# Squared leaky rectifier as two squares, a norm moved to ScalarE, scalings in one product

## The chip, the cores and the metric

One core of a Trainium2 chip runs the program. The metric is the device time of one execution in microseconds; the kernel before is given as the median of three runs, beside one profiled execution.

## What is computed

Two layers, each an attention-like part and an expert part, with a norm behind each. The change touches only the first part of layer 0, cut here to what matters:

```python
normed = _rms(x)
k, v, r = normed @ Wk.T, normed @ Wv.T, sigmoid(normed @ Wr.T)
# scan over the sequence of k*v -> wkv
x1 = x + mixer_scale * (r * wkv @ Wo.T)
h  = leaky_relu(_rms(x1) @ Wfc.T, negative_slope=0.5)
x2 = x1 + mlp_scale * (h * h @ Wmlp.T)
x3 = layernorm(x + x2)
# then layer 0's experts: 8, each token goes to 2 of them; then layer 1
```

x has 16 x 256 rows of 128; the hidden size of Wfc is 512. All of it is float32 here.

## The kernel before

Layer 0's first part runs over 8 chunks of 512 rows (4 tiles of 128). Its steps are software-pipelined by a table `AT` (line 34): the step numbered `u` is done for chunk k where u = 16 k + AT[name]. So a chunk's steps lie 16 apart, and the steps of up to six chunks are interleaved. Every engine runs the same list of slots in one written order (`program_order`, line 323) and does its own part of each slot; what it does in one slot it does in the order of the code. Nothing is reordered at run time: an instruction that waits holds everything behind it on its engine. From u = 64 on, slots of the experts of the first half of the rows stand between those of layer 0; then come the experts of the second half, the sums of the expert outputs, and layer 1's attention.

Seen modulo 16 from the large product `mlp` at step 2, TensorE does: logits and `mlp` (2), `fc` 1 (4), mix (6), `fc` 2 (7), the transpose of x (9), `fc` 3 (10), the transpose of x1 and ranks (12), k and v (13), the transpose of x3 (14), r (15), `fc` 0 of the next chunk (1). ScalarE does: half 0 (3), half 1 and exp (6), square 0 (7), half 2 (9), the squares of x1 for its norm and square 1 (10), the copy of xT (11), half 3 (12), square 2 (13), copies of x1T (14) and k (15), the squares of x, square 3 and the copy of x3T (0), the gate (1). VectorE: mixT (4), `x3_sums` (5), xn (6), x1 (8), the choice of two experts (8, 10), x3 (11), places (15), x1n (0), the scan (1), largest (2), and one `leaky` at 5, 8, 11 and 14. GpSimd: scatters of expert rows (2, 5, 8, 11; two DMAs each), the inverse roots (3, 9, 13) and `xx` (15).

The rectifier, for each of four 128-wide parts f of the hidden size: TensorE puts `fc` into PSUM bank 7 or 6 in turn (line 908); ScalarE writes its half to `z_half` (line 622, two buffers); VectorE takes the greater of the two, out of SBUF and PSUM, to `leaky` (line 759), which frees the bank; ScalarE squares that to `h_fc` (line 627). Then TensorE multiplies all four by `wmlp` into one bank, 16 products of 128x128x128 (line 922); one such product is two instructions, and so in the trace 32 a chunk.

The norm x3: VectorE adds the residual to `tmp` (line 763) and makes mean and variance (lines 766 to 769); GpSimd makes the inverse root (`inverse_root`, lines 475 and 477); VectorE subtracts and multiplies with both as scalars, four tiles a chunk (line 774). The two RMS scalings are four instructions each too (lines 714 and 754). `take` on TensorE (line 1995) holds a bank until its last reader has counted a semaphore up.

## Time and profile before

| | |
|---|---|
| median of 3 runs | 1436.43 us (1427.48 to 1438.81) |
| the profiled execution, its time | 1430.42 us |
| its span in the trace | 1428.6 us |
| TensorE busy | 1195.4 us (84%) |
| VectorE busy | 953.0 us (67%) |
| ScalarE busy | 733.5 us (51%) |
| GpSimd busy | 661.1 us (46%) |

The span is that of the instructions in the trace; the execution's time has 1.8 us around it. Engines in the rows: PE is TensorE (PEld its weight loads), DVE VectorE, ACT ScalarE, POOL GpSimd, SP the queue that issues most DMAs. Busy shares are over the whole span, of which layer 0's chunks are a small part and attention (from about 322 us on) the largest; the stretch of interest is read by itself.

### The profile page before, as it was taken

The numbers are of one execution on the slowest core, as the hardware profiler recorded it, in microseconds if no ns is written. First come the engines' busy times: TensorE is split into PE (matmuls) and PEld (weight loads), VectorE is DVE, ScalarE is ACT, GpSimd is POOL, SyncE is SP. The second block draws the span as 40 slices with busy tenths as digits, with TensorE's granted clock in tenths as the row PEclk, the third lists the DMA queues.
The fourth block names the chain that finished last, engine by engine and source line by source line (L and its number), as shares of the span: only waits on it lengthen the run. The fifth ranks groups of instructions, "written<-read, shape, count | busy, mean of one in ns | idle before, by whom it ended". The sixth has DMA issues, their size and how long they took to land.

```text
span 1428.6 us, 30595 instructions
## 1 busy us (share of the span) xinstructions
PE 1195.4 (84%) x11664; PEld 714.2 (50%) x11664; DVE 953.0 (67%) x2280; ACT 733.5 (51%) x1244; POOL 661.1 (46%) x1054
## 2 busy tenths in 40 slices
PE   5978786867676888999999989989999998999985
PEld 2545575654233344455545545455455555555554
DVE  4788542354468878787776768787786866747534
ACT  3654343334242466665655656566565655663541
POOL 2367442762268446364453626345462542543430
PEclk7999899987576899999998989999998999999887
DMA  9900366741010001101010110101011010110110
GB/s 341 356 16 32 114 206 201 223 137 42 16 35 25 15 7 42 33 14 38 10 45 3 44 32 15 37 11 45 20 28 33 14 45 4 44 42 18 23 36 8
DMA packets 69481, 87.53 MB, mean 61 GB/s; under 512 B 22062, under 2 KB 54104, under 8 KB 65880
## 3 DMA queue, kind: packets, MB, share of 16 engines
q1 hardware_dynamic: 65240, 77.18, 18.3%
q0 software_dynamic: 4096, 8.40, 1.9%
q8 instruction: 94, 1.54, 0.5%
q14 instruction: 51, 0.42, 0.1%
HBM read 52.16 MB, written 32.21 MB: 59 GB/s over the span
## 4 chain that ended last, share of the span: by engine, by line
PE 51%; DVE 27%; ACT 6%; issue 5%; POOL 4%; SPq 4%; DMA 2%; ACTq 0%; DVEq 0%; POOLq 0%
PE ps L1678 24%; PE ps L1758 11%; DVE mneg_e L1493 8%; PE ps L864 5%; PE ps L1781 4%; DVE mneg_l L1493 3%; POOL gathered L568 2%; DVE q L1548 2%; PE ps L960 2%; SPq L1137 2%; PE ps L1778 2%; DVE o_e L1591 1%; DVE x_all L847 1%; PE ps L1896 1%; DVE v_l L1668 1%
## 5 line engine op out<-in xcount | busy, mean ns | idle before, releaser
L1336 ACT ACTIVATE probs<-ps 128x1024 f32<-128x1024 f32 x384 | 389.3, 1023 | 231.5 <-PE ps L1678 230.8
L1493 DVE TENSOR_REDUCE mneg_e<-ps 128x2 f32<-128x512 f32 x512 | 335.8, 683 | 62.7 <-PE ps L1678 59.9
L1493 DVE TENSOR_REDUCE mneg_l<-ps 128x2 f32<-128x512 f32 x256 | 167.5, 685 | 63.9 <-PE ps L1678 62.4
L1678 PE MATMUL ps<-k_high,q_high 32*128 32x256 f16 x1024 | 163.6, 280 | 43.3 <-DVE mneg_e L1493 38.8
L1758 PE MATMUL ps<-probs,v_e 128*32 128x256 f32 x2048 | 139.7, 391 | 7.9 <-ACT v_e L1361 4.3
L1678 PE MATMUL ps<-q_high,k_high 32*128 32x256 f16 x1024 | 142.2, 278 | 3.6 <-ACT probs L1336 3.5
L1678 PE MATMUL ps<-q_low,k_high 32*128 32x256 f16 x1024 | 141.4, 275 | 0.0
L1678 PE MATMUL ps<-q_high,k_low 32*128 32x256 f16 x1024 | 140.4, 273 | 0.0
L1231 POOL CAST k_high<-k 128x512 f16<-128x512 f32 x64 | 39.8, 622 | 159.4 <-ACT k L1352 159.4
L1678 PE MATMUL ps<-kT,qT 32*128 32x256 f16 x512 | 76.7, 292 | 36.3 <-DVE mneg_l L1493 19.1
L1548 DVE SCALAR_TENSOR_TENSOR q<-ps,bq,pick 128x256 f32<-128x256 f32 x128 | 55.9, 478 | 72.5 <-PE ps L1678 72.5
L1276 POOL CAST routeT<-routeT 21x256 f16<-21x256 f32 x16 | 6.2, 387 | 195.0 <-ACT routeT L1424 195.0
L1678 PEld LDWEIGHTS ps<-k_high,q_high 32*128 32x128 f16 x1024 | 55.1, 93 | 82.4 <-DVE mneg_e L1493 58.2
L1289 POOL TENSOR_TENSOR on_e<-o_e,on_e 128x512 f32<-128x512 f32 x60 | 76.1, 1271 | 37.3 <-DMA on_e<-scratch_e 37.3
L551 POOL DMA_INDIRECT by_expert<-x_all,places x64 | 63.9, 998 | 52.0 <-DVE places L805 35.8
L1678 PEld LDWEIGHTS ps<-q_high,k_high 32*128 32x128 f16 x1024 | 48.9, 93 | 77.8 <-issue 52.0
L1758 PEld LDWEIGHTS ps<-probs,v_e 128*32 128x32 f32 x2048 | 54.0, 110 | 60.6 <-issue 22.7
L1758 PE MATMUL ps<-probs,v_l 128*32 128x256 f32 x1024 | 80.6, 440 | 1.1 <-DVE qkv L1561 0.3
L568 POOL DMA_INDIRECT gathered<-by_expert,places x64 | 62.2, 972 | 39.7 <-DMA by_expert<-y_tokens 22.6
L1678 PE MATMUL ps<-x5T,wq 128*128 128x256 f32 x256 | 74.7, 416 | 3.8 <-ACT k L1352 3.8
L1781 PE MATMUL ps<-x5T,wk 128*128 128x256 f32 x256 | 74.1, 417 | 0.0
L1236 POOL TENSOR_TENSOR k_low<-k,k_high 128x512 f16<-128x512 f32 x64 | 73.7, 1152 | 0.0
(245 smaller groups left out, 2501.5 us busy)
## 6 DMA issues: line engine op xcount, KB each, us to landing
by_expert<-expert_w SPq DMA_DIRECT2D x12, 1536.0 KB, 14.4
expert_w<-in_expert_w SPq DMA_DIRECT2D x48, 321.0 KB, 3.9
on_e<-scratch_e SPq DMA_DIRECT2D x60, 256.0 KB, 4.6
tokens<-by_expert SPq DMA_DIRECT2D x48, 128.0 KB, 2.6
by_expert<-y_tokens SPq DMA_DIRECT2D x48, 128.0 KB, 1.9
on_l<-scratch_l SPq DMA_DIRECT2D x128, 32.0 KB, 1.8
sums_l<-o_l SPq DMA_DIRECT2D x128, 2.0 KB
q_high<-shiftT_e SPq DMA_DIRECT2D x128, 2.0 KB
```

The costliest lines, as they stand in the source:

```text
L551: pool.indirect_dma_start(by_expert[g], bass.IndirectOffsetOnAxis(ap=places[:, n, at:at + 1], axis=0), x_all[:, at, :], None).then_inc(z.s ...
L568: pool.indirect_dma_start(gathered[:, k % 2, n, t, :], None, by_expert[g], bass.IndirectOffsetOnAxis(ap=places[:, n, k * CT + t:k * CT + t ...
L864: return pe.matmul(o, l, r, start=start, stop=stop)
L1231: pool.tensor_copy(k_high[:, b % 2, g], k32[:, g % 2]).then_inc(s.k16_ready, 1)
L1236: pool.tensor_tensor(k_low[:, b % 2, g], k32[:, g % 2], k_high[:, b % 2, g], ALU.subtract)\
L1289: pool.tensor_tensor(on_e[:, :, g], o_e[:, :, g], on_e[:, :, g], ALU.mult).then_inc(E.on_ready, 1)
L1336: act.activation(probs[:, probs_slot(r, i)].rearrange("p j s -> p (j s)"), s_banks(i).rearrange("p j s -> p (j s)"), ACT.Exp, scale=0.5 if ...
L1493: v.tensor_reduce(to, tiles(max_bank(k)), axis=AX, op=ALU.max, negate=True).then_inc(kind.max_used, 1)
L1548: last = v.scalar_tensor_tensor(q32[:, g % 2, c, :], x0[:, c * S:(c + 1) * S], bq[:, c, g:g + 1], pick[:, c, :], ALU.add, ALU.mult)
L1678: return pe.matmul(o, l, r, start=start, stop=stop)
L1758: last = pe.matmul(x1[ROW * j:ROW * (j + 1), to * S:(to + 1) * S], values, probs[:, probs_slot(r, first + 2 * t + j // 2), j % 2, c * S:(c ...
L1781: last = pe.matmul(x0[:, c * S:(c + 1) * S], wk[:, c, g, :], x5T[:, b % 2], start=False, stop=True, skip_group_check=True)
```

## The change

With z a part of `fc`, leaky(z) squared is z squared for z > 0 and (z/2) squared otherwise, and so (z/2)^2 + (sqrt(3/4) relu(z))^2. ScalarE now reads each part twice out of PSUM: Square with scale 0.5 to `z_square` (five buffers, since the product reads it a chunk later) and Relu with scale sqrt(0.75) to `z_half`; then it squares `z_half` to `h_fc` as before. VectorE's `leaky` is gone, and a bank is free with the second reading. TensorE adds the two squares up: 32 products a chunk in place of 16, into the same bank.

x3 is made on ScalarE as Identity with scale and bias, four tiles a chunk; GpSimd makes the bias (minus mean times inverse root) with one scaling and one product more (`norm_factors`). The two RMS scalings are one VectorE product each over 512 elements, with the root broadcast. New waits: half 1 on the product of the chunk before, each half on the square that last read its buffer, `x3_sums` on the x3 of the chunk before, x3 on GpSimd's factors from ScalarE.

```diff
+                def norm_factors(var, rstd, shift, mv, ready):
+                    steps[0] += 2
+                    pool.tensor_scalar(var, mv[:, :, 1], 1.0, LN_EPS, ALU.mult, ALU.add).then_inc(z.pool_step, 1)
+                    pool.tensor_scalar(shift, mv[:, :, 0], -1.0, None, ALU.mult)
+                    pool.wait_ge(z.pool_step, steps[0] - 1)
+                    pool.tensor_tensor(rstd, var, half[:, 0:CT], ALU.pow).then_inc(z.pool_step, 1)
+                    pool.wait_ge(z.pool_step, steps[0])
+                    pool.tensor_tensor(shift, shift, rstd, ALU.mult).then_inc(ready, 1)
...
-                        inverse_root(var0[:, 2, :], rstd0[:, 2, :], mv0[:, :, 1], 1.0, LN_EPS, z.x3_rstd)
+                        norm_factors(var0[:, 2, :], rstd0[:, 2, :], shift0[:], mv0[:], z.x3_rstd)
...
                             act.wait_ge(z.fc_ps, FC * k + f + 1)
+                            if k > 0 and f == 1:
+                                act.wait_ge(z.mlp_ps, k)
+                            act.activation(z_square[:, (FC * k + f) % (FC + 1), :], (x1, x0)[f % 2], ACT.Square, scale=0.5)
                             if FC * k + f > 1:
-                                act.wait_ge(z.leaky_ready, FC * k + f - 1)
-                            act.activation(z_half[:, f % 2, :], (x1, x0)[f % 2], ACT.Copy, scale=0.5).then_inc(z.half_ready, 1)
+                                act.wait_ge(z.hfc_ready, FC * k + f - 1)
+                            act.activation(z_half[:, f % 2, :], (x1, x0)[f % 2], ACT.Relu, scale=0.75 ** 0.5).then_inc(z.half_ready, 1)
...
-                            act.wait_ge(z.leaky_ready, FC * k + f + 1)
-                            act.activation(h_fc[:, f, :], leaky[:, f, :], ACT.Square).then_inc(z.hfc_ready, 1)
+                            act.wait_ge(z.half_ready, FC * k + f + 1)
+                            act.activation(h_fc[:, f, :], z_half[:, f % 2, :], ACT.Square).then_inc(z.hfc_ready, 1)
+                    for k in due(u, AT["x3"]):
+                        act.wait_ge(z.x3_rstd, k + 1)
+                        for t in range(CT):
+                            last = act.activation(rows(x_all, k, t), tmp[:, t, :], ACT.Identity, bias=shift0[:, t:t + 1],
+                                                  scale=rstd0[:, 2, t:t + 1])
+                        last.then_inc(z.x3_ready, 1)
...
-                        for t in range(CT):
-                            last = v.tensor_scalar(xn[:, 0, t, :], rows(x_all, k, t), rstd0[:, 0, t:t + 1], None, ALU.mult)
-                        last.then_inc(z.xn_ready, 1)
+                        v.tensor_tensor(xn[:, 0], rows(x_all, k), rstd0[:, 0, :].unsqueeze(2).broadcast_to([P, CT, D]), ALU.mult)                         .then_inc(z.xn_ready, 1)
...
-                        for t in range(CT):
-                            last = v.tensor_scalar(xn[:, 1, t, :], x1_sb[:, t, :], rstd0[:, 1, t:t + 1], None, ALU.mult)
-                        last.then_inc(z.x1n_ready, 1)
-                    for f in range(FC):
-                        for k in due(u, AT["leaky"][f]):
-                            v.wait_ge(z.half_ready, FC * k + f + 1)
-                            v.tensor_tensor(leaky[:, f, :], z_half[:, f % 2, :], (x1, x0)[f % 2], ALU.max).then_inc(z.leaky_ready, 1)
+                        v.tensor_tensor(xn[:, 1], x1_sb[:], rstd0[:, 1, :].unsqueeze(2).broadcast_to([P, CT, D]), ALU.mult)                         .then_inc(z.x1n_ready, 1)
...
                         v.wait_ge(z.mlp_ps, k + 1)
+                        if k > 0:
+                            v.wait_ge(z.x3_ready, k)
...
-                    for k in due(u, AT["x3"]):
-                        v.wait_ge(z.x3_rstd, k + 1)
-                        for t in range(CT):
-                            last = v.tensor_scalar(rows(x_all, k, t), tmp[:, t, :], mv0[:, t, 0:1], rstd0[:, 2, t:t + 1],
-                                                   ALU.subtract, ALU.mult)
-                        last.then_inc(z.x3_ready, 1)
...
-                            take((7, 6)[f % 2], z.leaky_ready, FC * k + f + 1)
+                            take((7, 6)[f % 2], z.half_ready, FC * k + f + 1)
...
                             for f in range(FC):
+                                mm(out_bank[:, t * D:(t + 1) * D], z_square[:, (FC * k + f) % (FC + 1), t * P:(t + 1) * P],
+                                   wmlp[:, f, :], start=f == 0, stop=False)
                                 last = mm(out_bank[:, t * D:(t + 1) * D], h_fc[:, f, t * P:(t + 1) * P], wmlp[:, f, :],
-                                          start=f == 0, stop=f == FC - 1)
+                                          start=False, stop=f == FC - 1)
```

## Rows read from the trace of the kernel before

**Rows 1.** Stretches between starts of line 763: length; busy us (instructions); clock; DMA; GB/s.
```profile
54.56:69.68 15.12, 13.61 (x75) 9.08 (x74) 11.65 (x33) 9.10 (x29) 5.71 (x7) 1.00 0.95 349
69.68:89.47 19.79, 15.71 (x79) 10.43 (x78) 16.37 (x57) 9.63 (x30) 10.53 (x11) 0.91 0.10 32
89.47:110.93 21.46, 15.39 (x79) 10.22 (x78) 20.04 (x57) 9.86 (x30) 16.94 (x29) 0.92 0.07 23
110.93:129.38 18.45, 15.55 (x79) 9.97 (x78) 16.14 (x56) 8.70 (x22) 14.67 (x16) 0.91 0.11 36
129.38:145.84 16.46, 13.26 (x70) 8.76 (x68) 15.25 (x60) 6.81 (x19) 11.04 (x13) 0.90 0.09 29
145.84:168.24 22.40, 14.29 (x64) 11.30 (x64) 9.67 (x43) 6.55 (x12) 10.92 (x12) 0.70 0.53 167
168.24:190.86 22.62, 18.59 (x124) 15.78 (x123) 10.86 (x45) 10.98 (x24) 9.00 (x10) 1.00 0.40 124
```

**Rows 2.** The chain of waits, 40 to 160 us: start, us, what.
```profile
110.93 0.70 DVE tmp L763
...
117.46 0.61 DVE leaky L759
...
148.70 1.04 POOL rstd L477
```

**Rows 3.** TensorE in order of time: start, us, line, what [idle before <-releaser].
```profile
54.36 1.02 PE L864 MATMUL ps<-x1T,wfc 128*128 128x512 f32 x2
...
65.83 3.82 PE L864 MATMUL ps<-wmlp,h_fc 128*128 128x128 f32 x32
69.48 1.02 PE L864 MATMUL ps<-x1T,wfc 128*128 128x512 f32 x2
...
157.86 1.09 PE L950 MATMUL ps<-ident,tokens 128*128 128x128 f32 x4 [4.48 <-DMA tokens<-by_expert]
...
162.02 6.19 PE L864 MATMUL ps<-wmlp,h_fc 128*128 128x128 f32 x32
```

**Rows 4.** ScalarE in order of time, 49 to 71 us.
```profile
49.93 0.64 ACT L627 ACTIVATE h_fc<-leaky 128x512 f32<-128x512 f32 x1
...
57.17 0.60 ACT L622 ACTIVATE z_half<-ps 128x512 f32<-128x512 f32 x1 [0.64 <-PE ps L864]
...
60.13 0.59 ACT L622 ACTIVATE z_half<-ps 128x512 f32<-128x512 f32 x1
60.62 0.62 ACT L627 ACTIVATE h_fc<-leaky 128x512 f32<-128x512 f32 x1
...
62.08 0.33 ACT L586 ACTIVATE junk<-x_all 128x128 f32<-128x128 f32 x1
...
63.27 0.63 ACT L627 ACTIVATE h_fc<-leaky 128x512 f32<-128x512 f32 x1
...
64.74 0.61 ACT L622 ACTIVATE z_half<-ps 128x512 f32<-128x512 f32 x1
70.54 0.60 ACT L622 ACTIVATE z_half<-ps 128x512 f32<-128x512 f32 x1 [5.20 <-PE ps L864]
```

**Rows 5.** Groups by line: form, count | busy us, mean ns | idle before, releasers.
```profile
L759 DVE TENSOR_TENSOR leaky<-z_half,ps 128x512 f32<-128x512 f32 x32 | 21.6, 679 | 5.4 <-ACT z_half L622 5.4
L754 DVE TENSOR_SCALAR xn<-x_sb,rstd 128x128 f32<-128x128 f32 x24 | 6.1, 324 | 0.1
L1368 ACT ACTIVATE x<-x_sum,shift,rstd 128x128 f32<-128x128 f32 x32 | 14.0, 486 | 11.5 <-POOL shift L1212 11.5
```

**Rows 6.** GpSimd in order of time, at 252 and 390 us.
```profile
252.23 1.00 POOL L568 DMA_INDIRECT gathered<-by_expert,places  x1 [22.59 <-DMA by_expert<-y_tokens]
...
390.58 0.20 POOL L1212 TENSOR_TENSOR shift<-shift,rstd 128x2 f32<-128x2 f32 x1
```

**Rows 7.** Single lines of VectorE: duration ns least/median/greatest, first and last start.
```profile
L774 DVE TENSOR_SCALAR x_all<-tmp,mv,rstd x32: 334/341/5175, 59.0 to 200.4; 128x128 f32<-128x128 f32 x32
...
L803 DVE TENSOR_TENSOR chosen_row<-chosen,row_of x8: 224/224/1168, 80.9 to 218.9; 128x64 f32<-128x64 f32 x8
```

More of the change, by code:

```diff
@@ L37 @@
     "xx": -65, "x1n": -64, "x1T": -52, "x1T_copy": -50, "fc": (-47, -44, -41, -38), "half": (-45, -42, -39, -36),
-    "leaky": (-43, -40, -37, -34), "h_fc": (-41, -38, -35, -32), "mlp": -30, "x3_sums": -27, "x3_rstd": -23, "x3": -21,
+    "h_fc": (-41, -38, -35, -32), "mlp": -30, "x3_sums": -27, "x3_rstd": -23, "x3": -21,
     "x3T": -18, "x3T_copy": -16, "logits": -14, "largest": -12, "exp": -10, "first": -8, "second": -6, "shares": -5,
@@ L103, in __init__ @@
         self.half_ready = sem("half_ready")
-        self.leaky_ready = sem("leaky_ready")
         self.hfc_ready = sem("hfc_ready")
@@ L416, in program @@
             x1_sb = sb0("x1_sb", [P, CT, D])
-            leaky = sb0("leaky", [P, FC, CS])
+            shift0 = sb0("shift0", [P, CT])
+            z_square = sb0("z_square", [P, FC + 1, CS])
             z_half = sb0("z_half", [P, 2, CS])
@@ L1954, in _ @@
             def _(pool):
-                root = pool_inverse_root(pool)
-                layer0, sums, attention = layer0_gpsimd(pool, root), sums_gpsimd(pool, root), attention_gpsimd(pool)
+                root, factors = pool_inverse_root(pool)
+                layer0, sums, attention = layer0_gpsimd(pool, root, factors), sums_gpsimd(pool, root), attention_gpsimd(pool)
                 for part, r, i in program_order():
```

4 lines of the change are left out of this document (2 added, 2 removed).

## The prediction

> **What bounds the kernel now.** I cut the span at the starts of line 763 (`tmp`, one per chunk, directly behind that chunk's last product) and read busy time, granted clock and DMA share of each piece [rows 1]. A chunk takes 15.12, 19.79, 21.46, 18.45 and 16.46 us (chunks 0 to 5, sum 91.28). VectorE is busy 11.65 of 15.12, but 15 to 20 us in the other four, so it looks like the bound. Then I read the chain of waits [rows 2]: in the fourth period it passes from `tmp` (110.93) over VectorE's routing steps to `leaky` (117.46), which frees the PSUM bank that TensorE's transposes want. So now VectorE does set those periods.
>
> The last view is each engine's order of time in the first period, where VectorE is light [rows 3, 4]. There the loop is another one. TensorE goes from `fc` 1 (54.36) to the same place one chunk on (69.48), which is 15.12. ScalarE starts the half of `fc` 2 at 57.17 and then works on in one run up to the half of `fc` 0 at 64.74. Behind it come logits and `mlp`, whose issue takes 65.83 to 69.48 = 3.65, and only then `fc` 1, for which ScalarE has waited 5.20 us (70.54). In sum: 2.81 (54.36 to 57.17), a ScalarE run of 7.57, 1.09 from half 0 to `mlp`, 3.65 of `mlp`: 15.12. Everything stands in engine order, so ScalarE rests during `mlp` and TensorE largely rests during ScalarE's run. What one adds to `mlp` and the other to its run adds up. That is the loop that the change lengthens.
>
> **The change part by part.**
>
> *Products.* `mlp` doubles: 16 more products, each two TensorE instructions, 32 more beside the 32 of 3.65 us [rows 3]. Same shapes, same weights operand: +3.65 per chunk. Nothing runs beside it that could hide it, since `fc` 1 stands behind it in TensorE's queue.
>
> *Second PSUM read on ScalarE.* Each `fc` result now costs two activations of 128x512 out of PSUM. Two such starts lie 0.49 apart (60.13 to 60.62, [rows 4]), so 4 x 0.49 per chunk. That of half 0 falls into ScalarE's rest during `mlp`, and that of half 1 still ends before `fc` 2 is there: 1.06 after `fc` 1 (69.48 to 70.54), plus 0.98, plus 0.62 for a square, makes 2.66 of the 2.81. Halves 2 and 3 are in the run: +0.98. Without that cover half 1 would cost 0.49 too.
>
> *Waits.* The half's wait for its buffer and the square's wait for its half are now ScalarE's own, so the stall on `leaky` goes. The bank is free 0.98 us after `fc`, which lets the transposes at 118 go early; what is late next is ScalarE's run. The wait for the product before (half 1) is over by order, as `fc` 1 stands behind that product. The wait of `x3_sums` for the x3 of the chunk before is a full period old.
>
> *x3 from VectorE to ScalarE.* The nearest row is the later norm on ScalarE, same form, 486 ns each [rows 5]. Bounds: 1.19 (four squares of that shape with their reads, 62.08 to 63.27, [rows 4]) and 4 x 0.486 = 1.94. Neighbours overlap by about 0.09, so I take 1.7. It stands in the run between the copy of xT and half 3: +1.7. Behind it wait half 3, the copies, the gate, and so logits and `mlp`. It waits for GpSimd's factors. Now the root is there at 148.70 + 1.04, which is 3.9 after that chunk's `tmp` at 145.84 [rows 1, 2]; with the new steps (below) 4.4. ScalarE gets to x3 2.81 + (60.13 - 57.17) + 0.49 = 6.3 after `mlp` [rows 3, 4], so the wait is covered by 1.9; if GpSimd is late with its scatters, which stand in front of the factors, I allow 1 us a period. x3 issues no DMA.
> The Trainium skill (ScalarE: Activation LUTs, Rules for kernel authors) says to put relu, max, add and multiply on VectorE and not on ScalarE, which speaks against this step. VectorE's x3 is 341 ns in the median, and 5175 ns once, when GpSimd cleared large tiles [rows 7]. By that rule x3 would stay where it was, and the sum would be 5 x 1.7 = 8.5 us less.
>
> *Factors on GpSimd.* A scaling and a product more; the later norm's product is 0.20 [rows 6]. With issue some 0.5 in front of each chunk's last two scatters. It counts once, where chunk 3's last scatters start the experts: +0.5.
>
> *Scalings in one product.* Four of line 754 are 4 x 0.324 [rows 5]; the nearest row for 512 elements with two inputs is line 759, 0.68. VectorE saves up to 0.6 twice a chunk, and with the four `leaky` (2.7) and x3 (1.4) 4 to 5. I count nothing for it: VectorE's work up to the expert mask is over 6.5 after `tmp` (110.93 to 117.46, [rows 2]), and ScalarE's run ends at 2.81 + 7.57 + 0.98 + 1.7 = 13.1. From below, the product could be held by GpSimd; line 803 took 1.168 in place of 0.224 while GpSimd added `xx` [rows 7]. The root that may run beside it is 1.04 [rows 2]; so 0 to 1.1 a period, and I take 0, as the row nearest in size (line 759) shows no hold.
>
> **The sum.** Period 0 to 1: 15.12 + 3.65 + 0.98 + 1.7 = 21.45. Periods 1 to 2 and 2 to 3 are the same, as routing and GpSimd's constants (now in the 21.46) have slack. In period 3 to 4 the four squares of x are gone (no chunk 8): 20.25. In 4 to 5 the xT and k copies and the gate too, 0.49 each like a half: 18.8. Together 103.4 against 91.28: +12.1.
> Before it, chunk 0's `mlp` and two activations in front of the square at 49.93: +4.6 (3.65 at least). Behind it, chunks 6 and 7 have their products between expert steps: 2 x 3.65 = 7.3. With the 0.5: 4.6 + 12.1 + 7.3 + 0.5 = 24.5.
> All of it reaches the end. TensorE waits 4.48 us at 157.86 for tokens that chunk 3's scatters release, and GpSimd's first gather at 252.23 waits 22.59 for the last expert output [rows 3, 6]; attention follows these in program order.
> The profiled execution took 1430.42, 6.0 below the median shown; the four executions known average 1433.3. So 1430.4 + 24.5 = 1454.9 beside the profile, and 1433.3 + 24.5 = 1457.8, my forecast, 1458.
>
> **Rivals.**
> *TensorE without gaps (not slower).* If VectorE's release lets TensorE run through, a period is TensorE's own work: 13.61 busy at full clock [rows 1] and 3.65: 17.26, five of them 86.3, 5.0 less than now. The clock would also stay up in the stretch at 0.70 (22.40 x 0.30 = 6.7). Then -5.0 - 6.7 + 3.65 + 7.3 = -0.8: 1433 in the mean of four, no change. For it: VectorE's load. Against: ScalarE's run already fills 7.57 of the 15.12 where VectorE is light. It decides once `mlp`'s end to the next `mlp` is under 91.28 / 5 - 7.30 = 11.0; I get 14.1.
> *The expert stretch swallows its two products.* From 145.84 to 190.86 TensorE is busy 32.9 of 45.0 us, with DMA at 0.53 and 0.40 [rows 1]. Then 7.3 goes: 1450. Against it: in the second of these stretches TensorE is busy 18.59 of 22.62.
> *The one product is held.* 1.1 a period between statistics and `x1`, on which ScalarE's squares wait: five times 5.5 and more, 1463. For it: line 803 [rows 7]. The Trainium skill (SBUF — State Buffer, Who interferes with whom) says that a VectorE instruction with two SBUF inputs waits for a GpSimd one that reads SBUF; by that, the product meets the root that starts at the same moment. Line 803 agrees.
> *The clock falls.* Chunk 6's `mlp` took 6.19 after TensorE's wait of 4.48, in a stretch granted 0.70, for 3.82 at full clock [rows 1, 3]. If the longer ScalarE runs do that to every doubled product: 2 x 2.4 x 8 = 38 more, 1496. Against: the first period, with the same gaps, was granted 1.00.
>
> **Numbers.** Forecast 0.57 (own range 1447 to 1468), no gaps 0.12, swallowed 0.15, held 0.08, clock 0.08. The range 1438 to 1478 leaves out half of the first rival, the clock and some tail, about 0.19. One per cent is what a measurement of this kernel tells from no change, here 14.3 us. Faster 0.07 (part of the first rival), same 0.22 (its rest, part of the second, the forecast's low end), slower 0.71.
>
> **What would show it.** `mlp` as 64 instructions of about 7.3 us in one piece. First full periods at 21 to 22 us from `tmp` to `tmp`. ScalarE without gaps from half 2 to the gate, about 10 us, and resting some 8 us during `mlp`; VectorE resting 5 us or more before `tmp`, no longer followed by stalls on banks. First expert transposes 16 to 17 us later, the first gather 24 later, attention of equal length. Wrong if periods stay under 19 (then ScalarE is not in the loop), if x3 waits for GpSimd more than 1 us, or if the shift at the first gather does not appear at the end.

## The result and the profile after

| | before | after |
|---|---|---|
| time, median (range), us | 1431.95 (1423.19 to 1438.81) | 1456.82 (1453.58 to 1462.71) |
| ratio, 95% interval | 1 | 1.0196 (1.0142 to 1.025) |
| the profiled execution: time; span, us | 1430.42; 1428.6 | 1457.26; 1455.3 |
| mean granted clock | 0.901 | 0.902 |
| TensorE instructions | 11664 | 11920 |
| start of `tmp` of chunk 0, of chunk 7; first gather, us | 54.56; 190.86; 252.23 | 58.97; 217.28; 279.22 |

The kernel before is now the median of four executions. The kernel became 2.0% slower (24.87 us between the medians; the interval of the ratio leaves 20 to 36 us); the forecast of 1458 and the median of 1456.82 lie 1.2 apart. The 256 new TensorE instructions are the 32 for each of eight chunks.

The stretches between the starts of `tmp` (now line 775), cut as in [rows 1], up to the first gather, and the rest (columns as there: length, busy us of TensorE, its weight loads, VectorE, ScalarE, GpSimd, granted clock, DMA share, GB/s):

```profile
58.97:79.85 20.88, 17.24 (x107) 12.66 (x106) 8.66 (x19) 12.45 (x37) 5.92 (x9) 1.00 0.53 183
79.85:100.73 20.88, 17.70 (x111) 13.11 (x110) 11.69 (x42) 12.56 (x38) 12.43 (x15) 1.00 0.06 20
100.73:121.61 20.88, 17.69 (x111) 13.11 (x110) 12.56 (x42) 12.57 (x38) 16.64 (x29) 1.00 0.05 16
121.61:141.65 20.04, 17.53 (x111) 13.10 (x110) 12.59 (x42) 11.62 (x30) 14.28 (x17) 1.00 0.11 37
141.65:164.25 22.60, 18.91 (x101) 15.59 (x100) 11.50 (x49) 10.05 (x27) 12.00 (x15) 0.77 0.07 23
164.25:188.50 24.25, 15.97 (x97) 12.14 (x96) 6.48 (x35) 9.37 (x20) 9.45 (x12) 0.79 0.48 148
188.50:217.28 28.78, 25.11 (x156) 22.08 (x155) 8.04 (x39) 13.64 (x31) 9.42 (x12) 0.88 0.33 101
217.28:279.22 61.94, 45.80 (x300) 40.32 (x298) 20.89 (x89) 23.50 (x55) 19.00 (x22) 0.95 0.67 197
279.22:1455.30 1176.08, 1007.62 (x10690) 575.14 (x10688) 799.69 (x1780) 625.80 (x936) 545.67 (x845) 0.90 0.14 36
```

Three things stand in it. First, three periods are equal to the hundredth, 20.88, while VectorE's load grows from 8.66 to 12.56 and GpSimd's from 5.92 to 16.64: neither of the two sets the period. Before, the same periods were 15.12, 19.79 and 21.46 [rows 1]. Secondly, all that is lost is lost before the first gather (27.0 us); behind it the stretch is 1176.08, and was 1428.60 - 252.23 = 1176.37. (These are single executions: two of one and the same code, e9 and e11 below, differ by 2.9 us at the first gather and by 5.0 behind it.) Thirdly, the clock is 1.00 in the full periods, where before had 0.91 and 0.92 in two of them, and falls in the fifth, to 0.77.

ScalarE in order of time, for the first period (the answer to [rows 4]):

```profile
61.58 0.60 ACT L631 ACTIVATE z_square<-ps 128x512 f32<-128x512 f32 x1 [0.15 <-PE ps L870]
62.08 0.60 ACT L634 ACTIVATE z_half<-ps 128x512 f32<-128x512 f32 x1
62.55 0.31 ACT L621 ACTIVATE junk<-x_sb 128x128 f32<-128x128 f32 x1
...
64.70 1.66 ACT L643 ACTIVATE x_all<-tmp,shift,rstd 128x128 f32<-128x128 f32 x4
66.25 0.58 ACT L631 ACTIVATE z_square<-ps 128x512 f32<-128x512 f32 x1
...
71.32 0.62 ACT L631 ACTIVATE z_square<-ps 128x512 f32<-128x512 f32 x1
...
80.71 0.60 ACT L631 ACTIVATE z_square<-ps 128x512 f32<-128x512 f32 x1 [8.28 <-PE ps L870]
```

TensorE beside it (the answer to [rows 3]):

```profile
58.77 1.02 PE L870 MATMUL ps<-x1T,wfc 128*128 128x512 f32 x2
...
72.42 0.47 PE L870 MATMUL ps<-wmlp,z_square 128*128 128x128 f32 x2
72.73 0.39 PE L870 MATMUL ps<-wmlp,h_fc 128*128 128x128 f32 x2
...
79.65 1.02 PE L870 MATMUL ps<-x1T,wfc 128*128 128x512 f32 x2
```

Read them as the prediction read before: `fc` 1 at 58.77, the half of `fc` 2 at 61.58 (2.81), a run of ScalarE up to the half of `fc` 0 at 71.32 (9.74), `mlp` at 72.42 (1.10), `fc` 1 again at 79.65 (7.23). Sum 20.88: the loop of two engines that wait for each other is still the one that sets the period, and ScalarE's rest behind it has grown from 5.20 to 8.28.

The expert stretch on TensorE, where the clock falls and two waits stand:

```profile
150.65 2.05 PE L870 MATMUL ps<-x1T,wfc 128*128 128x512 f32 x2 [1.32 <-ACT x1T L625]
152.49 1.71 PE L870 MATMUL ps<-wg,x3T 128*128 128x8 f32 x8
...
177.58 1.09 PE L958 MATMUL ps<-ident,tokens 128*128 128x128 f32 x4 [6.60 <-DMA tokens<-by_expert]
...
201.01 1.09 PE L874 MATMUL ps<-ident,x_all 128*128 128x128 f32 x4 [2.18 <-ACT x_all L643]
...
203.40 3.78 PE L968 MATMUL ps<-expert_w,h_moe 128*128 128x128 f32 x16 [0.44 <-ACT x3T L648]
```

The `fc` products at 150.65 take 2.05 where the ones at 58.77 take 1.02, so they ran at 1.2 GHz and not at 2.4 (the granted clock from 150 to 154 us is 0.50). Of `mlp` of chunk 5, behind them, 154.06 to 159.74 went at that level too: it took 9.99 us to the next `fc` at 164.05, and 7.23 in the first period.

### The profile page after: what moved, and what is told of

It reads as the page before. It is cut to its first block, busy times and chain, and to the rows that moved or that the text cites. A ratio compares the mean times of both kernels' runs of the same rounds, so it can differ in the third digit from the quotient of the medians.

```text
span 1455.3 us, 31052 instructions
## 1 busy us (share of the span) xinstructions
PE 1221.2 (84%) x11920; PEld 740.6 (51%) x11920; DVE 919.4 (63%) x2168; ACT 757.7 (52%) x1308; POOL 662.6 (46%) x1070
## 4 chain that ended last, share of the span: by engine, by line
PE 52%; DVE 24%; ACT 8%; issue 6%; SPq 4%; POOL 4%; DMA 3%; ACTq 0%; DVEq 0%; POOLq 0%
PE ps L1686 22%; PE ps L1766 10%; DVE mneg_e L1501 8%; PE ps L870 7%; PE ps L1789 4%; DVE mneg_l L1501 3%; PE ps L968 2%; SPq L1145 2%; POOL gathered L577 2%; DVE q L1556 2%; PE ps L1786 2%; DVE o_e L1599 1%; DVE x_all L853 1%; PE ps L1904 1%; DVE v_l L1676 1%
## 5 line engine op out<-in xcount | busy, mean ns | idle before, releaser
L560 POOL DMA_INDIRECT by_expert<-x_all,places x64 | 63.7, 995 | 37.8 <-DVE places L811 21.2
```

The costliest lines, as they stand in the source:

```text
L560: pool.indirect_dma_start(by_expert[g], bass.IndirectOffsetOnAxis(ap=places[:, n, at:at + 1], axis=0), x_all[:, at, :], None).then_inc(z.s ...
```

## The experiments

Each is timed against the kernel before on the same chip. "First gather" is the start of GpSimd's first gather in its trace (252.23 before, 279.22 after); all the work of layer 0 lies ahead of it, so it shows a few us that the whole time, which spreads by 1 to 2% from execution to execution, doesn't. It has a spread of its own: e9 and e11, the same code, have it 2.9 apart, and so a difference under about 3 us there says little.

| run | full periods | fifth (clock) | first gather | ratio, 95% |
|---|---|---|---|---|
| after | 20.88 x3 | 22.60 (0.77) | 279.22 | 1.0196 (1.0142 to 1.025) |
| e1 x3 on VectorE | 19.36 x3 | 19.86 (0.83) | 268.65 | 1.0098 (1.0049 to 1.0148) |
| e2 four scalings | 20.89, 20.88, 20.88 | 22.64 (0.77) | 280.28 | 1.0254 (1.019 to 1.0318) |
| e3 16 products | 17.31, 17.31, 17.32 | 19.09 (0.73) | 259.79 | 1.005 (1.001 to 1.0091) |
| e4 one reading | 20.05 x3 | 20.54 (0.83) | 271.41 | 1.0216 (1.0146 to 1.0286) |
| e8 rests filled | 20.88, 20.89, 20.88 | 18.33 (1.00) | 280.33 | 1.0204 (1.0122 to 1.0287) |
| e9, e11 early scatters | 20.88 x3 | 21.71 (0.76), 21.80 (0.77) | 271.48, 274.39 | 1.0213 (1.0125 to 1.0301), 1.0221 (1.0177 to 1.0265) |
| e12 = e1 and e9 | 19.37, 19.37, 23.37 | 21.08 (0.76) | 268.97 | 1.0125 (1.0086 to 1.0163) |
| before | 15.12, 19.79, 21.46 | 16.46 (0.90) | 252.23 | 1 |
| e5 before, x3 on ScalarE, one scaling | 16.47, 20.52, 18.74 | 15.07 (1.00) | 254.15 | 0.9976 (0.9923 to 1.0028) |
| e6 before, bank free early | 15.13, 18.61, 20.35 | 15.76 (0.89) | 247.35 | 1.0039 (1.0 to 1.0077) |
| e7 = e5 and e6 | 16.48, 18.42, 19.54 | 18.10 (0.72) | 256.06 | 1.0018 (0.9974 to 1.0063) |
| e10 = e7, early scatters, rests filled | 16.48, 17.23, 20.19 | 18.45 (0.81) | 258.39 | 1.0114 (1.0058 to 1.0171) |

**The parts of the change, undone one at a time (e1 to e4).** The theory was the prediction's: a period is ScalarE's run plus `mlp`, so what is taken out of either comes off the period one for one, and the scalings are worth nothing. The rivals were hidden work on one engine or the other.

e1, x3 back on VectorE, GpSimd with the plain root:

```diff
-                    for k in due(u, AT["x3"]):
-                        act.wait_ge(z.x3_rstd, k + 1)
...
-                            last = act.activation(rows(x_all, k, t), tmp[:, t, :], ACT.Identity, bias=shift0[:, t:t + 1],
...
+                    for k in due(u, AT["x3"]):
+                        v.wait_ge(z.x3_rstd, k + 1)
...
+                            last = v.tensor_scalar(rows(x_all, k, t), tmp[:, t, :], mv0[:, t, 0:1], rstd0[:, 2, t:t + 1],
+                                                   ALU.subtract, ALU.mult)
```

> The last norm is back on VectorE, the rest is as in the changed kernel. Theory (x3 lies in ScalarE's run, and the run and mlp wait for each other): the three full periods go from 20.88 to about 19.3 us (the step from the start of x3 to half 3 is 1.55), five periods lose 1.5 each, and TensorE's wait of 2.18 us for x3 behind the experts' work on ScalarE goes too. Total 8 to 10 us less than the changed kernel: about 1447 where before is 1432, ratio near 1.012. Rival (VectorE needs what ScalarE gave back; x3 is hidden either way): periods stay within 0.3 of 20.88, total within 2 us of the changed kernel, ratio 1.018 to 1.022. Second question: in the fifth period (22.60 us, clock at 0.65 in its last part) the clock stays at 0.9 or more if TensorE's wait of 1.12 us for x3 was what let it fall; if not, the fifth period stays above 21.

```profile
58.93:78.29 19.36, 17.22 (x107) 12.66 (x106) 9.77 (x23) 10.93 (x33) 5.48 (x7) 1.00 0.56 188
...
135.67:155.53 19.86, 17.70 (x101) 14.38 (x100) 12.46 (x52) 8.53 (x23) 11.70 (x13) 0.83 0.09 30
155.53:182.13 26.60, 18.46 (x97) 14.80 (x96) 7.53 (x38) 7.96 (x16) 8.99 (x10) 0.74 0.43 135
```

These are stretches between starts of `tmp`, as above. It is 1.52 less in each full period, against the 1.55 from the start of x3 (64.70) to the next reading (66.25): ScalarE's step comes off whole, though VectorE gets x3 back. First gather 10.6 earlier, the ratio as expected within its interval. The second question came out between its two answers: the fifth period's clock is 0.83, under 0.9, but the period is 19.86, not above 21. TensorE's wait of 1.12 for x3 is 0.42 there, and the clock fell even so.

e2, four scalings in place of one product, twice:

```diff
-                        v.tensor_tensor(xn[:, 1], x1_sb[:], rstd0[:, 1, :].unsqueeze(2).broadcast_to([P, CT, D]), ALU.mult)                         .then_inc(z.x1n_ready, 1)
+                        for t in range(CT):
+                            last = v.tensor_scalar(xn[:, 1, t, :], x1_sb[:, t, :], rstd0[:, 1, t:t + 1], None, ALU.mult)
```

> The changed kernel with the two scalings as four instructions each, as before. Theory (the one product was worth nothing, since VectorE rests before each tmp): periods 20.88 within 0.2, total within 2 us of the changed kernel, ratio 1.018 to 1.022. Rival (the one product is held by GpSimd's root): periods up to 1.1 us shorter, total up to 5 us less, ratio 1.015 to 1.018. Third possibility (the one product saves what it saves on VectorE, 0.5 twice a chunk, on the path): periods 0.5 to 1.0 longer, total 3 to 8 us more, ratio 1.022 to 1.026.

The full periods stay within a hundredth, so the scalings are off the path both ways. The first gather is 1.1 later, less than one code differs from itself, and the ratio's interval (1.019 to 1.0318) holds that of no difference; the third possibility, longer periods, is out.

e3, the products of `z_square` left out, and with them a part of the output:

```diff
-                                mm(out_bank[:, t * D:(t + 1) * D], z_square[:, (FC * k + f) % (FC + 1), t * P:(t + 1) * P],
-                                   wmlp[:, f, :], start=f == 0, stop=False)
```

> The changed kernel with the products of z_square left out of mlp, so that part of the output is missing; all of ScalarE's work is kept. Theory (mlp stands alone on the loop): full periods 20.88 - 3.6 = 17.3, start of the loop 3.6 earlier, chunks 6 and 7 up to 3.6 each: total 25 to 29 us less than the changed kernel, about 1430, ratio 0.995 to 1.003. Rival (TensorE has gaps that take the products): periods 19 or more, total less than 12 us lower, ratio above 1.011.

```profile
55.42:72.73 17.31, 13.67 (x75) 9.08 (x74) 8.66 (x20) 12.46 (x37) 5.93 (x9) 1.00 0.82 294
...
107.36:129.25 21.89, 17.33 (x79) 12.10 (x78) 12.55 (x42) 11.73 (x30) 17.37 (x20) 0.84 0.12 39
129.25:148.34 19.09, 15.41 (x69) 12.08 (x68) 11.51 (x49) 10.06 (x27) 12.03 (x15) 0.73 0.09 28
148.34:172.57 24.23, 15.38 (x65) 11.56 (x64) 6.47 (x34) 9.38 (x20) 9.47 (x12) 0.65 0.47 148
```

The three full periods confirm `mlp` as the largest term: 20.88 - 17.31 = 3.57. (The first `tmp` is 3.55 earlier, but that place varies: after, e8, e9 and e11, the same code up to there, have it at 58.97 to 60.02.) But the fourth period is 1.85 longer than with 32 products, at a clock of 0.84 where that had 1.00. It begins on ScalarE:

```profile
115.34 1.65 ACT L643 ACTIVATE x_all<-tmp,shift,rstd 128x128 f32<-128x128 f32 x4 [2.13 <-POOL shift L486]
```

In periods this short x3 waits 2.13 us for GpSimd's factors, which stand behind six scatters (104.67 to 113.44). TensorE then rests 1.47 for x3 and 1.72 for the copy of k, and from 120 to 126 us it is granted 0.57 and 0.50. So two things take a part of the gain back, a wait for GpSimd that the longer chunks cover and the clock behind it; how much each would take alone no run shows. The first gather comes 19.4 earlier and not 25 to 29, and the ratio of 1.005 lies above the expected 0.995 to 1.003, which its interval still touches.

e4, one reading of each `fc` result on ScalarE; `z_square` isn't computed, and `mlp` takes `h_fc` twice, so that the output differs:

```diff
-                            act.activation(z_square[:, (FC * k + f) % (FC + 1), :], (x1, x0)[f % 2], ACT.Square, scale=0.5)
...
-                                mm(out_bank[:, t * D:(t + 1) * D], z_square[:, (FC * k + f) % (FC + 1), t * P:(t + 1) * P],
+                                mm(out_bank[:, t * D:(t + 1) * D], h_fc[:, f, t * P:(t + 1) * P],
```

> The changed kernel without the first reading of each fc result on ScalarE: z_square isn't computed and mlp multiplies by h_fc twice, so the output differs; 32 products are kept. Theory (two of the four readings stand in ScalarE's run): full periods 20.88 - 0.97 = 19.9, total 5 to 7 us less than the changed kernel, ratio 1.014 to 1.017. If the readings of halves 0 and 1 are not hidden either: 20.88 - 1.95 = 18.9, total 10 us less, ratio near 1.012. Rival (the readings are hidden, VectorE or GpSimd are next): 20.6 or more, total within 2 us, ratio 1.018 to 1.022.

Periods of 20.05: 0.83 less, not 0.97. ScalarE's order of time has the missing 0.14. Of the two readings in the run one is gone whole (0.48); without the other the squares behind it must wait for `x1`, so that the step from the reading to the squares is 60.78 - 60.17 = 0.61 where it was 62.55 - 62.08 = 0.47 with both.

```profile
60.17 0.60 ACT L631 ACTIVATE z_half<-ps 128x512 f32<-128x512 f32 x1 [0.64 <-PE ps L867]
60.78 0.31 ACT L621 ACTIVATE junk<-x_sb 128x128 f32<-128x128 f32 x1
```

The first gather is 7.8 earlier. The ratio, 1.0216 (1.0146 to 1.0286), can't tell that from nothing.

The three parts together account for the loop: 20.88 - 3.57 - 1.52 - 0.83 = 14.96, and the one full period of before that has this form took 15.12.

**Where x3 costs nothing (e5).** The kernel before, with two parts of the change, and its own rectifier:

```diff
-                        inverse_root(var0[:, 2, :], rstd0[:, 2, :], mv0[:, :, 1], 1.0, LN_EPS, z.x3_rstd)
+                        norm_factors(var0[:, 2, :], rstd0[:, 2, :], shift0[:], mv0[:], z.x3_rstd)
...
-                            last = v.tensor_scalar(rows(x_all, k, t), tmp[:, t, :], mv0[:, t, 0:1], rstd0[:, 2, t:t + 1],
+                            last = act.activation(rows(x_all, k, t), tmp[:, t, :], ACT.Identity, bias=shift0[:, t:t + 1],
...
-                            last = v.tensor_scalar(xn[:, 1, t, :], x1_sb[:, t, :], rstd0[:, 1, t:t + 1], None, ALU.mult)
+                        v.tensor_tensor(xn[:, 1], x1_sb[:], rstd0[:, 1, :].unsqueeze(2).broadcast_to([P, CT, D]), ALU.mult)                         .then_inc(z.x1n_ready, 1)
```

> The kernel before with two of the three parts of the change: x3 on ScalarE with GpSimd's factors, and the scalings in one product; the rectifier and its 16 products stay as before. Theory (what x3 costs depends on the engine that sets the period): in the first period, which ScalarE's run sets, 15.12 + 1.55 = 16.7; in the three periods that VectorE sets (19.79, 21.46, 18.45) up to 2.6 us less each, down to 17 to 19; first gather 3 to 6 us earlier than 252.23, ratio 0.995 to 1.000. Rival (x3 costs on ScalarE's run whatever the rest is, as between the changed kernel and the one with x3 back on VectorE): 1.5 us more per period, first gather 8 to 10 later, ratio 1.005 to 1.008.

```profile
54.48:70.95 16.47, 13.87 (x75) 9.10 (x74) 9.98 (x24) 10.62 (x33) 5.91 (x9) 1.00 0.93 338
70.95:91.47 20.52, 16.73 (x79) 11.12 (x78) 15.04 (x46) 11.40 (x34) 11.77 (x14) 0.83 0.04 14
91.47:110.21 18.74, 15.71 (x79) 10.54 (x78) 16.74 (x46) 10.97 (x34) 15.88 (x29) 0.91 0.07 22
110.21:127.25 17.04, 14.14 (x79) 9.45 (x78) 14.70 (x47) 9.90 (x26) 13.97 (x17) 1.00 0.10 35
```

The two edits cost 1.35 in the first period, which ScalarE's run sets, and give 2.72 and 1.41 in the third and fourth, which in before wait for VectorE. The third has a reason of its own. There VectorE's four x3 of before stood beside GpSimd's clearing of its large tiles and took 5.95 (the 5175 ns of [rows 7]), and TensorE waited for them:

```profile
102.65 1.09 PE L868 MATMUL ps<-ident,x_all 128*128 128x128 f32 x4 [3.13 <-DVE x_all L774]
```

In e5 no x3 stands on VectorE to be held, and that alone can give the 2.72. The second period is 0.73 longer, at a clock of 0.83 for 0.91; the stall on `leaky` (3.12) is still in it. Up to the sixth `tmp` that is 3.5 us gained (142.32 against 145.84); the expert stretch gives it back, and the first gather is 1.9 later. In time it is no difference. The theory stands for the first, third and fourth period; it failed for the second (20.52, where 17 to 19 were expected) and for the first gather (expected 3 to 6 earlier).

**The bank (e6, e7).** In before, `leaky` reads PSUM behind VectorE's routing steps and so holds the bank that TensorE's transposes want [rows 2]. The change frees it after ScalarE's readings. e6 does that, with `leaky` read from SBUF alone and four buffers for `z_half`; the time of one `leaky` stays (684 ns in the median, 679 in before):

```diff
-                            act.activation(z_half[:, f % 2, :], (x1, x0)[f % 2], ACT.Copy, scale=0.5).then_inc(z.half_ready, 1)
+                            act.activation(z_half[:, f, :], (x1, x0)[f % 2], ACT.Copy, scale=0.5).then_inc(z.half_ready, 1)
...
-                            v.tensor_tensor(leaky[:, f, :], z_half[:, f % 2, :], (x1, x0)[f % 2], ALU.max).then_inc(z.leaky_ready, 1)
+                            v.scalar_tensor_tensor(leaky[:, f, :], z_half[:, f, :], 2.0, z_half[:, f, :], ALU.mult, ALU.max).then_inc(z.leaky_ready, 1)
...
-                            take((7, 6)[f % 2], z.leaky_ready, FC * k + f + 1)
+                            take((7, 6)[f % 2], z.half_ready, FC * k + f + 1)
```

> The kernel before, where leaky reads z_half alone (from SBUF, four buffers) and the PSUM bank of fc is free after ScalarE's one reading, as it is after the second in the changed kernel; nothing else. Theory (leaky behind the routing steps held the bank, and this stretched periods 2 to 4): they go from 19.79, 21.46 and 18.45 to 17 to 19, the first period stays within 0.3 of 15.12, first gather 4 to 8 earlier. Rival (VectorE's work itself sets these periods, 16 to 20 us busy, and the bank was only where it showed): they stay within 0.5, first gather within 2 us of 252.23.

The second to fourth periods go to 18.61, 20.35 and 17.20, some 1.2 less each, and the first gather comes 4.9 earlier. TensorE's waits in the second period, of before and then of e6:

```profile
77.95 0.86 PE L868 MATMUL ps<-ident,xn 128*128 128x128 f32 x4 [3.12 <-DVE leaky L759]
```

```profile
76.40 0.38 PE L864 MATMUL ps<-mask,upper 128*128 128x32 f32 x2 [2.38 <-DVE mask L790]
```

The stall on the bank goes, and behind it stands one on VectorE's expert mask: both hypotheses are half right. In the third period x3 too comes out from beside GpSimd's clearing (1.11 for 5.95), so that its gain isn't the bank's alone. The 4.9 at the gather don't appear at the end, where the ratio is 1.0039 (1.0 to 1.0077). e7 is the kernel before with the diffs of e5 and e6.

> Both edits on the kernel before: x3 on ScalarE, scalings in one product, the bank free after ScalarE's reading; 16 products. Theory: all periods fall to ScalarE's run, 16.5 to 17.5; five of them 84 against 91.3; first gather 6 to 8 us earlier, about 1426 where before is 1432, ratio 0.994 to 0.997. Rival (the clock takes it back: TensorE rests longer between its products, and the clock falls in more periods): a granted clock under 0.95 in two or more full periods, first gather within 2 us of 252.23.

The rival's clock came true, with 0.81 in the fourth period, 0.72 in the fifth and 0.65 in the sixth; its first gather did not, which is at 256.06, 3.8 later than in before and later than with either edit alone. And the clock isn't all: the third period has 1.00 and takes 19.54, with VectorE busy for 18.50 of it, and in the fourth x3 waits 1.75 for GpSimd's factors.

**The clock of the fifth period (e8).** Idle transposes in three of TensorE's waits, the first of the three shown:

```diff
+                def keep_busy(dst, n):
+                    for i in range(n):
+                        pe.transpose(dst[:, (i % CT) * P:(i % CT + 1) * P], ident[:], ident[:])
...
+                        if k == 3:
+                            keep_busy(tokens_bank, 7)
                         pe.wait_ge(z.mask_ready, k + 1)
```

> The changed kernel with 24 idle transposes on TensorE (7, 9 and 8) put into three of its waits in the fifth period (before the expert mask, before x3, before x1T); they compute nothing that is used. Theory (the fifth period took 22.60 and not 18.8 because TensorE's rests ahead of 150 us let the clock fall to 0.5 up to 159.7): with the rests filled the clock of this period is 0.95 or more, mlp of chunk 5 takes 7.2 and not 9.9, the period 18.3 to 18.9, 3.7 to 4.3 less. Rival (the clock falls there whatever TensorE does, after some 100 us at full speed): clock again 0.75 to 0.83, period 22 to 23. Whether the rest of the expert stretch keeps the gain is open: first gather 0 to 4 earlier than 279.2.

```profile
142.92:161.25 18.33, 16.48 (x117) 13.29 (x116) 11.48 (x49) 10.06 (x27) 12.01 (x15) 1.00 0.09 30
161.25:188.02 26.77, 17.86 (x97) 14.19 (x96) 6.48 (x34) 9.38 (x20) 9.44 (x12) 0.74 0.43 134
```

The period is 18.33 at a clock of 1.00, 4.27 less than the 22.60 at 0.77. So the fall came from TensorE's rests ahead of it, and it was the whole of what this period had over the forecast's 18.8. Eight of the 24 transposes, those ahead of x1T, fall into the fourth period and not the fifth; that went from 20.04 to 20.82, so that the two together gain 3.49. The next row shows where it went: 26.77 at 0.74, where after had 24.25 at 0.79. TensorE then waited 7.24 for the first tokens (6.60 after), ran the logits behind that wait in 1.71 and `mlp` of chunk 6 in 8.81 (179.01 to 187.82), where after took 7.23 (181.07 to 188.30). The first gather is 1.1 later than after's, where 0 to 4 earlier were expected. To fill these rests moved the loss and did not remove it.

**GpSimd's order (e9, e11, e12).** The first expert transposes come 13.3 behind `tmp` of chunk 5, since the last scatters of chunk 3 stand behind chunk 5's factors in GpSimd's queue, and those wait for that `tmp`. The first factor and the scatter, in after:

```profile
166.35 0.19 POOL L481 TENSOR_SCALAR var<-mv 128x4 f32<-128x4 f32 x1 [8.11 <-DVE mv L781]
...
168.33 1.08 POOL L560 DMA_INDIRECT by_expert<-x_all,places  x1 [0.16 <-issue]
```

```diff
-    "ranks": -4, "places": -1, "scatter": (2, 5, 8, 11),
+    "ranks": -4, "places": -1, "scatter": (2, 5, 8, 8),
```

> The changed kernel with the last two scatters of each chunk issued by GpSimd at step 8 and not at step 11, that is ahead of the factors of a later chunk and not behind them; nothing else. Theory (the expert stretch starts 13 us behind tmp of chunk 5 only because chunk 3's last scatters stand behind chunk 5's factors in GpSimd's queue: scatter 168.33, tokens in 177.58): the last scatter moves to about 159, the tokens land near 168, the wait of 6.60 us ahead of the first expert transposes goes (under 1), these start near 171, first gather 4 to 7 us earlier than 279.2, ratio 1.013 to 1.017. Rival (what holds the expert stretch lies elsewhere, in its weights or its own steps, or the clock takes the gain back as it did with the filled rests): first gather within 2 us of 279.2, ratio 1.018 to 1.022.

The stretch of e9 that answers to 24.25, then its TensorE:

```profile
164.09:181.11 17.02, 14.44 (x97) 11.07 (x96) 6.48 (x34) 9.17 (x20) 9.01 (x12) 1.00 0.69 207
```

```profile
171.38 0.66 PE L958 MATMUL ps<-ident,tokens 128*128 128x128 f32 x4 [0.92 <-DVE places L811]
```

In the trace it is as expected: last scatter at 159.69, the wait of 6.60 gone, the stretch 17.02 at full clock, the first gather 7.7 earlier. The timed ratio did not follow. e11 is the same kernel (the diff of e9), timed in more rounds.

> The kernel with the early scatters once more, in more rounds, since its first gather came 7.7 us earlier (271.48 against 279.22) while its timed ratio (1.0125 to 1.0301) was too wide to show 0.5%. Theory (what is gained at the first gather reaches the end): ratio 1.011 to 1.017. Rival (attention or the second group of experts gives it back): ratio 1.018 to 1.024, with a stretch from first gather to the end that is 5 us or more longer than the 1176.1 of the changed kernel.

The trace repeats the stretch (17.02 at 1.00), the first gather is at 274.39; the ratio is 1.0221 (1.0177 to 1.0265), inside the rival's expectation. The rival's own sign, a longer stretch behind the first gather, is not there (1167.21). That trace belongs to the shortest of its executions, 1443.57 with the longest at 1464.30. So it stays open whether the others lose the gain ahead of the gather or behind it. Every execution has its mean granted clock on record, and the six go from 1443.57 at 0.914 to 1464.30 at 0.899: by and large a longer one is one at a lower clock, and 5 us can't be seen in that spread.

e12 is the changed kernel with the diffs of e1 and e9.

> The changed kernel with x3 back on VectorE and the early scatters, both. Theory (the two are terms of one sum: ScalarE's run, and GpSimd's order ahead of the expert stretch): full periods 19.36 again, the wait for the first tokens under 1.5 us, first gather at 260 to 263 (268.65 less 6 to 8), ratio 1.003 to 1.009. Rival (x3 on VectorE had already shortened the expert stretch, so that the two overlap): first gather at 266 to 269, ratio 1.009 to 1.012.

The first gather is at 268.97, as the rival had it, but not for its reason: the third period went to 23.37. (The ratio, 1.0125, lies above both ranges; its interval reaches into both.) VectorE's x3 in it:

```profile
103.59 5.74 DVE L778 TENSOR_SCALAR x_all<-tmp,mv,rstd 128x128 f32<-128x128 f32 x4
```

With the scatters moved, GpSimd cleared its large tiles (from 105.32 on, one of them 2.67) just beside these four, which took 5.74, and TensorE waited 3.25 for them. It is what [rows 7] showed as 5175 ns. With x3 on ScalarE no run shows the like, but in none does x3 stand beside the clearing; other instructions of ScalarE that do (k's copy 0.60, a reading 0.62 in after, 110 to 115 us) are not longer for it.

**All remedies on before (e10).** e7 with the early scatters of e9 and idle transposes:

```diff
+                        if 0 < k < 5:
+                            keep_busy(tokens_bank, 9)
                         pe.wait_ge(z.mask_ready, k + 1)
...
+                        if q == 0:
+                            for i in range(45):
+                                pe.transpose(tokens_bank[:, (i % CT) * P:(i % CT + 1) * P], ident[:], ident[:])
                         pe.wait_ge(ex.tokens_loaded[q % 3], DMA * PAIR * (q // 3 + 1))
```

> The kernel before with x3 on ScalarE, the scalings in one product and the bank free after ScalarE's reading (all as in the run with both), the scatters at step 8, and idle transposes in TensorE's waits: 9 ahead of each expert mask of chunks 1 to 4, 45 ahead of the first expert tokens. Theory (with the bank free and x3 gone, only the clock of 0.65 to 0.81 kept the periods at 18): clock 0.95 or more from 90 to 175 us, periods 3 to 6 at 15.5 to 17.5, 0.65 of the sixth gone, first gather at 242 to 248, about 6 to 10 us earlier than before (252.23), ratio 0.992 to 0.997. Rival (VectorE's 15 to 18 us set the periods, and the transposes only hide that): periods stay at 18 to 19.5, first gather at 251 to 256, ratio 0.998 to 1.003.

The second period is 17.23 at full clock, as wanted. But the third is 20.19, at full clock too, and the fourth and fifth are 21.61 and 18.45 at 0.92 and 0.81. ScalarE's x3 in the third and fourth:

```profile
95.26 1.65 ACT L641 ACTIVATE x_all<-tmp,shift,rstd 128x128 f32<-128x128 f32 x4 [3.23 <-POOL shift L487]
...
116.51 1.65 ACT L641 ACTIVATE x_all<-tmp,shift,rstd 128x128 f32<-128x128 f32 x4 [4.27 <-POOL shift L487]
```

It waits for GpSimd four times, 11.6 us in all (three times in e7, 3.1). The scatters at step 8 stand ahead of the factors (in the third period six in a row up to 92.93, the factors from 93.00): what helped in e9, where the chunks are long enough and x3 never waits, costs here. So e10 adds a wait of its own and doesn't test whether only the clock kept e7's periods long; e7's third, 19.54 at full clock, speaks against that. The first gather, 258.39, lies behind both ranges, and the ratio above both. The 45 transposes ahead of the tokens ran in good part at the low level (0.50 up to 161 us):

```profile
157.13 7.30 PE L962 MATMUL ps<-ident 128*128 128x128 f32 x45 [1.99 <-DVE places L813]
```

Behind them no wait for tokens is left; what of the 7.30 us was cost isn't shown, but e9, with the same early scatters, had a wait of 0.92 at this place. No version here beats the kernel before by what its measurement can tell.

## Why the prediction was right, and which steps were not

| part | forecast | measured (traces) |
|---|---|---|
| up to chunk 0's `tmp` | +4.6 | +4.41 |
| three full periods (56.37 before) | +7.98 | +6.27 |
| period 3 to 4 (18.45) | +1.80 | +1.59 |
| period 4 to 5 (16.46) | +2.34 | +6.14 |
| `tmp` 5 to `tmp` 7 (45.02) | +7.3 | +8.01 |
| from there to the first gather | 0 | +0.57 |
| the factors ahead of the scatters | +0.5 | 0 |
| first gather to the end | 0 | -0.29 |
| sum | +24.5 | +26.7 |

**What bounds it.** Right. That a period is `fc` 1 to half 2, ScalarE's run, 1.1 and `mlp` was read from one period of before, the one in which VectorE is light. After the change every full period has this form, and e1, e3 and e4 move it by what they take out of its terms. That VectorE set the other periods was right in part: in the second it held the bank (e6), and the third waited 3.13 us for an x3 that GpSimd's clearing held (e5).

**Products.** 3.65 forecast, 3.57 in e3. `mlp` stands in one piece of 7.23.

**Second reading.** 0.98 forecast for the run. The measured run is 9.74; 7.57 + 0.97 + 1.55 is 10.09. The missing 0.35 was a wait: in before ScalarE started the reading at 57.17 [rows 4] and the squares of `x1` only at 57.96, 0.79 later and not 0.47, since `x1` wasn't ready:

```profile
57.96 0.31 ACT L612 ACTIVATE junk<-x_sb 128x128 f32<-128x128 f32 x1 [0.20 <-DVE x_sb L744]
```

The second reading fills 0.32 of this, nearly all of the 0.35. The step that failed is the term "halves 2 and 3 are in the run: +0.98". It priced by duration what partly lay in a wait. e4 shows the same wait coming back.

**x3.** 1.7 forecast, 1.55 by position and 1.52 by e1. It never waited for GpSimd (the last factor ends 84.10, 4.25 after `tmp`; 4.4 was forecast), and starts 1.5 behind it; 1.9 was forecast. How thin that is e3 shows, where the chunk is 3.57 shorter and one x3 waits 2.13. What the step lacked is the expert stretch: there x3 stands in ScalarE's queue behind the experts' activations, and TensorE waits 2.18 for it at 201.01, against 0.47 for VectorE's x3 in before. In e1 no such wait is left.
The Trainium skill (ScalarE: Activation LUTs, Rules for kernel authors) gives add and multiply to VectorE and so would have left x3 there. For the changed kernel e1 agrees, with 10.6 us at the first gather (8.5 were worked out). e5 bounds it: on the kernel before, the same move with the one product made three of five periods shorter, one of them (the third) by taking x3 from beside GpSimd's clearing.

**Scalings in one product.** Nothing, as forecast, but two sizes in that step were wrong. VectorE saves 0.18 with the one product for `xn` (0.84 for four, 0.66 for one), not 0.6. The mean of 324 ns of line 754 [rows 5] has held instructions in it; in e2 the same instruction has a median of 275 and a greatest of 1291. And the other product is held. VectorE and GpSimd at the same time:

```profile
65.23 1.75 DVE L769 TENSOR_TENSOR xn<-x_sb,rstd 128x512 f32<-128x512 f32 x1 [3.07 <-POOL rstd L477]
```

```profile
65.17 1.27 POOL L551 TENSOR_TENSOR x_all<-x_sb,x_all 128x512 f32<-128x512 f32 x1
```

The median of the eight is 1.73, the least 0.68. So the rival "held product" had its mechanism right, at the `xx` addition and not at the root, and its price wrong: four scalings in the same place take 1.87, and the transposes that read the product stand 12 steps later in the order, so nothing waits. The row that the prediction took for no hold, line 759, reads one of its inputs from PSUM, so it could not tell. By the Trainium skill (SBUF — State Buffer, Who interferes with whom) a VectorE instruction with two SBUF inputs meets a GpSimd one that reads SBUF; this trace agrees.

**Factors.** +0.5 forecast, 0 found: the scatter behind them starts 4.08 after `tmp` of chunk 5 (168.33 - 164.25), and 4.10 before (149.94 - 145.84). The new steps are there, but in before the root began 0.48 later after `tmp` (148.42, and 166.35 in after), behind scatters of its own queue.

**The clock.** The largest miss. The sum priced period 4 to 5 at 18.8 for full clock, and e8 shows 18.33 there; the trace had 0.77 and 22.60. The rival "the clock falls" priced this for all eight products and got 0.08; it happened to one. Part of it was paid before: then chunk 6's `mlp` ran at the low level (6.19 in a stretch at 0.70, [rows 1, 3]), and after it runs at full clock, so there `mlp` up to the next `fc` grew by 1.21 (6.02 to 7.23) and not by 3.65, and its whole stretch by 1.85. The loss moved forward by a chunk. In the stretch behind that it shows again: of its +6.16, 3.57 are the products, 1.83 line 968 at the low level (3.78 for 1.95), 1.2 three smaller groups beside it (1.09, 1.06 and 2.23 for 0.63, 0.66 and 1.89), 1.7 the wait for x3, less a wait of 2.28 for the places of a chunk that only before has (182.19).

**The other rivals.** "TensorE without gaps" was to decide under 11.0 from `mlp` to `mlp`; it is 13.65 (58.77 to 72.42). "The expert stretch swallows its two products" is out with +8.01 for 7.3.

**The signs named.** Right: one piece of `mlp`, ScalarE's run (61.58 to 71.46, 9.9) and its rest of 8.28, VectorE's rest of 5.71 and 6.83 before `tmp`, no stall on `leaky` (banks still stall TensorE, for ScalarE's reading, by 0.3 to 1.0 from 145 us on), attention of equal length. A little off: 20.88 for 21 to 22. Off: the first expert transposes 19.7 later and not 16 to 17, the first gather 27.0 and not 24. The end came out close by some luck: terms too large (2.4 in the full periods, the fourth and the factors) stand against terms too small (3.8 in the fifth period, 1.3 behind it), and the 1.2 us between forecast and median are far less than the measurement can tell. The first row is luck in part as well, as the same code has chunk 0's `tmp` up to 1.05 later in other runs.

## What to carry to other kernels

Where two engines wait for each other in a fixed order, price a change by what it adds to each one's piece of the loop, whatever their busy shares are; here a VectorE that was 15 to 20 us busy in most periods got 3.0 to 7.5 us lighter, and the kernel got slower. Price an added instruction against the wait it may fall into, not by its duration alone. Before moving work ahead in a queue, ask what stands behind it there: the early scatters took a wait of 6.60 away in one kernel and made four of 11.6 together in another, since x3's factors came behind them. And where TensorE has rests, keep a term for the clock with its own place: in e8 filled rests gained 4.27 in one period, and the next stretch grew by 2.52. Parts taken out singly need not add up to the whole change: they gave 19.4, 10.6 and 7.8 us at the first gather, 37.8 together and more than its 27.0. Without them the kernel would not be the one before, since `leaky` and what it holds stay out: worked out, the three full periods would take 3 x 14.96 = 44.9, and they took 56.37.

## What the runs showed of the hardware beyond that

- Less work on TensorE can come with a longer stretch: the fourth period of e3 has 32 TensorE instructions fewer than that of after (79 for 111) and takes 21.89 at a clock of 0.84, for 20.04 at 1.00. 2.13 us of it are a wait of x3 for GpSimd that the longer chunks cover; TensorE's low level (0.57 and 0.50 from 120 to 126 us) comes behind it.
- Ahead of the fall in the fifth period TensorE had 1.28 of 4.00 us busy (146 to 150 us), and the clock of the next 4.00 was 0.50:

```profile
146.00:150.00 4.00, 1.28 (x9) 0.94 (x8) 3.22 (x17) 4.00 (x13) 3.54 (x5) 0.95 0.10 33
150.00:154.00 4.00, 3.35 (x10) 2.35 (x11) 3.65 (x12) 2.59 (x6) 3.21 (x4) 0.50 0.10 33
```

- e9 and e11 are the same code. Their periods agree to 0.1 us, but from the last `tmp` to the first gather they take 61.98 and 64.49, and behind it 1172.22 and 1167.21. A trace of this kernel shows a tenth of a us in the loop, not under about 3 us at the first gather, and a single whole time not 0.5%.
